# Attention stage: context loaded at the head of its round, loads of x spread over rounds, another order at the stage's end

## The reference, cut to what matters

```python
def _L0_xattn_ref(x, latents, Wq, Wkv, Wo, ...):     # 64 sequences, 128 tokens, 256 wide, 16 heads of 64
    xn, ln = _layernorm(x, ...), _layernorm(latents, ...)
    q  = ln @ Wq
    kv = concatenate([xn, ln], axis=-2) @ Wkv         # keys and values of context and latents
    w  = softmax(q k^T / 8); out = w @ v
    return out @ Wo                                   # added to x
...
# then: experts (shared and routed feed-forward), DTW alignment, quantised convolution feed-forward
```

## Time and profile before

| what | value |
|---|---|
| three timed runs | 3246.82, 3253.71, 3256.96 us; median 3253.71 us |
| the profiled execution | 3256.71 us, of which its span (first to last instruction) is 3255.0 us |
| attention stage in it | from 0 to about 1740 us |
| TensorE's mean granted clock over the span | 0.948 of full speed |

### The profile page before, as it was taken

The page is one execution under the profiler, slowest core; times in us unless marked ns, Lnnn a source line. Parts: engine busy times, 40 slices in busy tenths (PEclk is TensorE's granted clock), DMA queues, the critical chain, the costliest instruction groups (busy, mean ns, idle before and its releaser), DMA issues. The chain is left out here.

```text
span 3255.0 us, 61553 instructions
## 1 busy us (share of the span) xinstructions
PE 2894.3 (89%) x21067; PEld 2485.9 (76%) x21070; DVE 2358.4 (72%) x5003; ACT 1762.5 (54%) x4520; POOL 2007.4 (62%) x1983
## 2 busy tenths in 40 slices
PE   6999999999999999999996999999999963078987
PEld 5888888888888888888885888888888851046765
DVE  5667676666667666766655878787877759889997
ACT  5566566656565666666563333323333326169997
POOL 5778787878787787878783333433333320058887
PEclk9999999999999999999998999999999975589999
DMA  7565555555556555565553121212121242011111
GB/s 212 109 106 103 104 106 107 106 105 107 106 110 108 106 104 109 104 107 109 104 108 109 41 66 47 73 43 74 46 70 50 59 77 50 0 34 40 46 40 40
DMA packets 704757, 272.16 MB, mean 84 GB/s; under 512 B 606168, under 2 KB 667328, under 8 KB 704448
## 3 DMA queue, kind: packets, MB, share of 16 engines
q1 hardware_dynamic: 704448, 268.23, 39.0%
HBM read 120.16 MB, written 13.73 MB: 41 GB/s over the span
## 5 line engine op out<-in xcount | busy, mean ns | idle before, releaser
L840 POOL COPY attention_probT<-attention_planesT 128x1024 uint16<-128x1024 uint16 x512 | 677.2, 1368 | 266.2 <-PE attention_turns L421 193.1
L528 ACT ACTIVATE attention_prob<-attention_turns,attention_neg_max 128x256 f32<-128x256 f32 x1024 | 468.6, 483 | 303.4 <-DVE attention_neg_max L681 302.8
L1431 POOL TENSOR_TENSOR experts_hidden_lo<-experts_weighed,experts_hidden_hi 128x512 fp32r<-128x512 f32 x192 | 255.1, 1329 | 530.9 <-ACT experts_hidden_hi L1184 530.9
L831 POOL COPY attention_planes<-attention_prob 128x1024 uint16<-128x1024 uint16 x512 | 527.1, 1060 | 20.5 <-ACT attention_prob L528 20.5
L681 DVE TENSOR_REDUCE attention_neg_max<-attention_turns 128x2 f32<-128x512 f32 x512 | 318.1, 683 | 216.0 <-PE attention_turns L406 216.0
L382 PE MATMUL attention_turns<-kv_hi,wkv 128*128 128x512 f32 x1024 | 374.6, 406 | 0.0
L1184 ACT ACTIVATE experts_hidden_hi<-experts_weighed 128x512 fp32r<-128x512 f32 x192 | 121.4, 632 | 404.3 <-DVE experts_weighed L1321 404.3
L350 PE MATMUL attention_turns<-wkv,kv_hi 128*128 128x512 f32 x1024 | 315.5, 389 | 1.9 <-ACT attention_prob L528 1.9
L421 PE MATMUL attention_turns<-attention_probT,attention_v 128*64 128x128 f32 x4096 | 253.7, 277 | 2.1 <-issue 2.1
L517 ACT COPY attention_v<-attention_turns 128x512 f32<-128x512 f32 x256 | 150.3, 589 | 187.2 <-PE attention_turns L350 187.1
L697 DVE TENSOR_TENSOR attention_turns<-attention_turns,attention_attT_lo 128x512 f32<-128x512 f32 x128 | 139.8, 1092 | 139.3 <-DMA attention_attT_lo<-inverse_rows 133.4
(11 more groups left out here) (297 smaller groups left out, 8696.7 us busy)
## 6 DMA issues: line engine op xcount, KB each, us to landing
attention_attT_lo<-inverse_rows SPq DMA_DIRECT2D x256, 128.0 KB, 2.9
experts_spread<-shares SPq DMA_DIRECT2D x256, 128.0 KB, 3.0
attention_ctx<-in_ctx SPq DMA_DIRECT2D x32, 256.0 KB, 3.0
attention_planesT<-attention_planes SPq DMA_TRANSPOSE x512, 3.2
experts_far_ctxT<-in_ctxT SPq DMA_DIRECT2D x32, 256.0 KB, 3.4
weights_ctx<-in_ctx SPq DMA_DIRECT2D x16, 512.0 KB, 3.8
out<-conv_x_out SPq DMA_DIRECT2D x15, 512.0 KB, 2.8
x_all<-in_x SPq DMA_DIRECT2D x7, 1024.0 KB, 8.9
```

Source lines behind the costliest of these rows:

```text
L528: made = act.activation(prob[n % 2][:, h, :], bank_of("s", 2 * n + e)[:, m * 256:(m + 1) * 256], ACT.Exp, bias=neg_max[:, n % 2, 2 * e + m ...
L831: pool.tensor_copy(planes[n % 2][:, g, :, :], words.rearrange("p (c b) -> p b c", b=2)).then_inc(planes_made, 1)
L840: pool.tensor_copy(words.rearrange("p (c b) -> p b c", b=2), planesT[:, g, :, :]).then_inc(joined, 1)
L1431: pool.tensor_tensor(hid_lo[n % 3][:, :], weighed[n % 2], hid_hi[n % 3][:, :].bitcast(F32), ALU.subtract).then_inc(hid_split, 1)
```

## The change

SP loads the context of pair `p + 2` right behind `load_inverses`, ahead of the transposes of unit `2u - 1`. The seven big loads of x are issued one to a round, at the ends of rounds 0 to 6; the wait for the staged weights stands in round 5, ahead of load 7. The router's weights and the bias are loaded in round 7. In round 128 SP issues the first four loads of the experts' weights after `load_inverses(126)` and ahead of the transposes of unit 255; the other four stay at the end. ScalarE makes all high parts of these weights after its loop, behind `high_heads(127)`. VectorE makes the low parts of the first four in round 129, behind `low_heads(127)`. No instruction is added or removed.

```diff
-            for n in range(2, FREE_LOADS):
-                load_x(n)
+            def load_following(first, last):
+                for i in range(first, last):
+                    src, place, hi, lo = following[i]
+                    sp.dma_start(place, src).then_inc(stage_loaded[i // KD], 16)
+
             for u in range(ROUNDS + LAG):
                 p, i = divmod(u, QUADS)
                 if u >= LAG:
                     load_inverses(u - LAG)
+                if i == 3 and p + 2 < PAIRS:
+                    load_ctx(p + 2)
+                if u == ROUNDS:
+                    sp.wait_ge(params_loaded, 48)
+                    projections_made(sp)
+                    load_following(0, SHARED_PARTS)
                 if 0 < u <= ROUNDS:
                     for g in range(2):
                         turn_planes(2 * u - 1, g)
                 if u < ROUNDS:
-                    if i == 3 and p + 2 < PAIRS:
-                        load_ctx(p + 2)
                     store_inverses(u)
                     for g in range(2):
                         turn_planes(2 * u, g)
-                if not u:
-                    sp.wait_ge(w_split, WO)
-                    for n in range(FREE_LOADS, len(X_LOADS)):
-                        load_x(n)
+                if u + 2 < len(X_LOADS):
+                    if u + 2 == FREE_LOADS:
+                        sp.wait_ge(w_split, WO)
+                    load_x(u + 2)
+                if u + 2 == len(X_LOADS):
                     sp.dma_start(shared.router_w[:, :, :], router.rearrange("(k p) n -> p k n", p=P)
                                  ).then_inc(params_loaded, 16)
                     sp.dma_start(shared.bias_w[:, :], bias).then_inc(params_loaded, 16)
-            sp.wait_ge(params_loaded, 48)
-            projections_made(sp)
-            for i, (src, place, hi, lo) in enumerate(following):
-                sp.dma_start(place, src).then_inc(stage_loaded[i // KD], 16)
+            load_following(SHARED_PARTS, len(following))
@@ ScalarE
-                if u == ROUNDS:
-                    for i in range(GATE_PARTS):
-                        high_following(i)
-            for i in range(GATE_PARTS, len(following)):
+            for i in range(len(following)):
                 high_following(i)
@@ VectorE
                 if u == ROUNDS:
                     low_first()
+                if u == ROUNDS + 1:
                     for i in range(SHARED_PARTS):
                         low_following(i)
```

## The result

The changed kernel takes 3177.84 us (median of 4 runs, 3173.84 to 3180.45) against 3253.01 us before: ratio 0.977, 95% interval 0.9751 to 0.9788. That is a gain of 75 us where 97 were forecast, inside the stated range, 21 us above the point. The profiled execution has a span of 3178.7 us, 76.3 less than before, and is the longest of the four runs (3180.45 us).

The account below looks back on a forecast made before the run. TensorE, 89% busy, was held mainly by VectorE waiting for the context's late DMA. Gains of 90.2 + 2.3 - 0.6 + 5.3 = 97.2 us from 3256.7 gave 3159.5, or 3157 us against the timed median; range 3138 to 3192.

Parts of the forecast that it names:

- the sum: Whole kernel: 90.2 for periods + 2.3 for round 3 - 0.6 for x + 5.3 at the end = 97.2 us gained.
- the start: Rounds before round 4: 2.3 us from the thirtieth stall, in round 3, and 1.44 us from clearing x from the queue.
- What bounds the kernel: Attention stage: TensorE waits 29 times, 64.2 us, at the output product because VectorE waits for the context's DMA.
- The forecast 0.85 us a period: Rounds 4 to 119: part of the 3.11 us a period, busy time at a lower clock behind some stalls.
- 29 x (52.73 - 49.62) = 90.2: Rounds 4 to 119: each of 29 four-round periods shrinks from 52.73 us to the last period's 49.62.
- the model: The period from round 120, which loads and measures no context: 49.62 us, taken as typical of the others.
- nothing moves relative to TensorE's scores: Rounds' start on VectorE: argument that shorter rounds would not make it late, since TensorE's scores start its round.
- the rival: VectorE becomes the bound of quads 0 and 1, leaving 41 of 90 us; gain about 48, time 3206; chance 0.12.
- A new wait of TensorE for scores in most periods: Sign of being wrong: TensorE newly waiting for scores or turned inputs would mean VectorE is the bound.
- 2 us lost against 1.44 won: Loads of x: 1.44 us of TensorE's wait saved in the start, 2 us lost by misses in rounds 3 and 7.
- the slack: Round 31's pattern: with heads' scaling slipped by a load, the low part ends near 449, ahead of TensorE's 449.4.
- The end: 5.3 us: End of stage: next stage's first matmul at about 1734.3 instead of 1739.69, as scaling no longer waits behind weights.

Follow-up runs that it names:

- measuring later: Kernel before, all DMAs where they were; VectorE measures the context only behind the low parts of heads, queries and keys: 3172.06 us, ratio 0.9756.
- Keys first: Changed kernel, with VectorE's low part of the second keys in quad 0 ahead of normalising the context: 3159.72 us, ratio 0.9714 against the kernel before.
- x as before: Changed kernel, with loads of x, router weights and bias back where they were before the change: 3174.61 us, ratio 0.9759 against the kernel before.
- the place behind the sums: Changed kernel, with big loads of x issued a round later, behind inverse sums and context, ahead of the transposes: 3183.38 us, ratio 0.9782.
- x in halves: Changed kernel, with seven 1 MB loads of x cut into fourteen of 512 KB, one a round: 3176.95 us, ratio 0.9766 against the kernel before.

## Why the prediction was right, and where it was too large

Span against span the gain is 76.3 us where the sum had 97.2. The 21 us between them are 13.9 us in rounds 4 to 119, 0.9 in rounds 120 to 123, 3.5 at the end of the stage and 3.8 in the rest of the program, less 1.1 that the start gave more than forecast.

- **What bounds the kernel.** Right. The 29 waits of TensorE and the 29 of VectorE were one thing, and it is gone: 76 us from the context's move alone.
- **How it is dear.** Shown by measuring later: with the DMA where it was, and VectorE still waiting 51.4 us for it, TensorE's stall disappears when nothing that TensorE needs stands behind the wait.
- **The clock.** The forecast 0.85 us a period came back: busy time for the same matmuls fell by 27 us between rounds 4 and 120 (0.95 a period), some 22 of them by the clock, and the granted clock is 1.00, the 2.4 GHz level, where windows behind 13 of the 29 stalls had shown 0.50.
- **The term that was mis-sized: 29 x (52.73 - 49.62) = 90.2.** It measured 76.4. 28 of the 29 periods take 49.91 us, 0.29 more than the model: 8.1 us. The first takes 55.42: 5.8 us. Together 13.9, which is the gap.
- **The 8 us: "nothing moves relative to TensorE's scores".** This sentence, written against the rival, was wrong. VectorE is the bound of quad 0 in about half the periods: idle time ahead of the scores rose from 6.5 us in 20 places to 19.6 us in 18. "A new wait of TensorE for scores in most periods" was the prediction's own sign for this rival, whose price it put at 49 us. Keys first shows that it is VectorE's normalising, by moving it behind the keys, and that the cost is 17 us. The sum missed only 8 of them, and that is luck: I had one period as the model, which had its quad 0 at 12.07 us, where quad 0 takes from 12.06 to 14.04 in rounds 8 to 119 of the changed kernel, but which lost 0.5 us in its quad 1 (12.97 us, 12.50 in a clean one).
- **The 6 us: the loads of x.** I put 2 us lost against 1.44 won. The slip of the inverse sums was 3.0 us, as forecast. What was wrong is the slack: it was read from round 31, a quad 3, and used for all rounds. In rounds 4 and 5, quads 0 and 1, where VectorE normalises, the slip cost 2.6 and 1.6 us; in round 6 nothing; in round 7, a quad 3, 1.9 where 1 was forecast. Together 6.1 us, and 1.1 more in round 8. In the start round 2 gave 1.2 us (13.70 against 14.89 with x as before), but rounds 1 and 3 took 1.3 and 0.9 more. The Trainium skill says that a queue's descriptors are taken in ring order (DMA: Bandwidth & Descriptors, Queues, rings and completion order). The trace agrees: sums that stood behind 1 MB landed in 6.2 and 6.0 us, where the median is 3.0.
- **The end: 5.3 us.** It measured 1.8 in this pair of traces, 2.9 on average over all kernels. The wait behind the weights went as forecast: from issue to scaling it takes 4.6 us instead of 9.3. The missing 3.5 us have two parts. The last scaling came 1.7 us later after the first score of round 124 than laid out, mostly because the last weighing took 3.68 us at the low clock instead of 1.97. With x as before, whose end is the same, it took 1.97, and the stretch was 0.6 us shorter (76.8).
- **The end, two engines side by side.** The other 1.9 us lie between the scaling and the next stage: the forecast left out that the new order puts VectorE's two subtractions beside GpSimd's, where they took 4.88 us instead of 2.35; leaving GpSimd out gives back 1.5. SBUF — State Buffer, SBUF: two separate sides, of the Trainium skill, says that a VectorE instruction with two inputs in SBUF and a GpSimd one that reads SBUF exclude each other for whole instructions. The trace agrees: VectorE's first took 1.60 us and ended 1.1 us after GpSimd's first; GpSimd's second took 3.31 us instead of 2.36, and VectorE's second 3.35 us instead of 1.22, ending 1.1 us after GpSimd's second. These are the times of two engines taking turns.
- **Not settled.** Why the rest of the program took 3.8 us longer in the profiled execution. The five other kernels with exactly the same end took 1515.0 to 1518.2 us for it, so it is no price of the change that I could name. And why quad 0 is late in some periods and not in others. The trace shows what goes with it: in the 29 rounds of quad 0 from 8 to 120, VectorE waited 1.5 us or more for the inverse sums in 17, of which 16 took 13.0 us or more, and at most 1.4 us in the other 12, which took 12.06 to 12.39. Why the sums come late in just those rounds is open; no run changed that alone.

## What to carry to other kernels

A load whose waiter stands in front of other work has to be issued by its waiter's turn, or the waiter has to be moved behind that work; they were worth 76 and 79 us here, with intervals that overlap, and the second needs no change to the queue. Idle time of the issuing engine in front of a critical step isn't room for a big transfer: in rounds 4 to 15, eleven loads of half a megabyte cost as much as four of a whole one, and over rounds 0 to 11 the place behind the sums cost 4.2 us more than the place ahead of them. Slack belongs to a kind of round: the same slip of 3 us cost nothing in quad 2 and 2.6 us in quad 0. When a model period is taken from the trace, take its spread too: one period hid a wait that half of them would have. And when work is moved up, look at what it will now run beside.

## What the runs showed of the hardware

- One load of 1 MB ahead of a 128 KB load in the same queue moved the small one's landing from a median of 3.0 us to 5.5 to 6.3 (rounds 2 to 6 of the changed kernel); one of 512 KB moved it to 4.0 to 4.8 (x in halves, rounds 2 to 7). Two transposes behind such a load of 1 MB took 5.05 us to issue instead of 2.63.
- Subtracting 128 x 1024 numbers takes VectorE 1.2 us; two of them took 4.88 us beside GpSimd's, and GpSimd's two took 5.64 instead of the 4.69 before, when VectorE's came after them.
- In the kernel before, the clock fell to 0.50 behind 13 of the 29 stalls at the output product (1.79 to 2.79 us long) and not behind the other 16 (1.71 to 2.82 us), so the length of the stall alone does not decide it. Without these stalls rounds 8 to 119 of the changed kernel show 1.00.
